# One pool of eight PSUM banks, scores in one block, and a gather product from split parts

## The reference

```python
x = _layernorm(x + attention(x, adj, adj, Wq, bq, Wk, bk, Wv, bv, Wo, bo))
# second layer, per head: h is x
Wh = jnp.einsum('bni,hoi->bhno', h, W) + bW[None, :, None, :]
e = jnp.einsum('bhno,hop->bhnp', Wh, attn)
scores = jnp.einsum('bhnp,bhmp->bhnm', e, Wh)
A_mat = jnp.tanh(jnp.where(adj[:, None, :, :], scores, 0.0))
hp = jax.nn.relu(jnp.einsum('bhnm,bhmo->bhno', A_mat, Wh))
cat = jnp.transpose(hp, (0, 2, 1, 3)).reshape(hp.shape[0], hp.shape[2], -1)
ha = cat @ A_w.T
hf = h @ fc_w.T
coeff = jax.nn.sigmoid(hf @ g1_w.T + ha @ g2_w.T + gbias)
x = _layernorm(x + hf * coeff + ha * (1.0 - coeff))
```

## Time and profile before

| | |
|---|---|
| median of 3 runs | 1156.95 us (1155.82 to 1157.34) |
| the profiled execution | 1157.57 us, of which the span is 1155.8 |
| granted TensorE clock, mean | 0.991 |
| TensorE busy | 1123.6 us (97%), 9756 matmul records |
| weight loads busy | 912.6 us (79%) |
| VectorE busy | 697.1 us (60%) |
| ScalarE busy | 511.6 us (44%) |
| GpSimd busy | 255.2 us (22%) |

### The profile page before, as it was taken

The page is one execution under the profiler, slowest core; times in us unless marked ns, Lnnn a source line. Parts: engine busy times, 40 slices in busy tenths (PEclk is TensorE's granted clock), DMA queues, the critical chain, the costliest instruction groups (busy, mean ns, idle before and its releaser), DMA issues.

```text
span 1155.8 us, 24597 instructions
## 1 busy us (share of the span) xinstructions
PE 1123.6 (97%) x9756; PEld 912.6 (79%) x9756; DVE 697.1 (60%) x1321; ACT 511.6 (44%) x908; POOL 255.2 (22%) x232
## 2 busy tenths in 40 slices
PE   6899999999999999999999999999999999999996
PEld 5778888787887878888787888878788787887774
DVE  6655665757556675665757566575765667566543
ACT  4444363534536253453625436353453625445241
POOL 1622131222212222131122213122221222211100
PEclk9999999999999999999999999999999999999998
DMA  7001000010000001000010100001000100100000
GB/s 248 16 7 41 19 22 20 18 40 18 25 29 24 19 18 40 18 20 19 18 40 18 40 18 20 19 18 40 18 21 24 33 19 18 40 19 3 1 19 18
DMA packets 26699, 32.58 MB, mean 28 GB/s; under 512 B 4400, under 2 KB 23344, under 8 KB 26288
## 3 DMA queue, kind: packets, MB, share of 16 engines
q1 hardware_dynamic: 26672, 32.19, 8.5%
HBM read 23.80 MB, written 8.39 MB: 28 GB/s over the span
## 4 chain that ended last, share of the span: by engine, by line
PE 94%; DVE 2%; POOL 2%; ACT 1%; issue 0%; DMA 0%; POOLq 0%; DVEq 0%; SPq 0%
PE bankB L344 20%; PE bankB L345 19%; PE bankB L346 19%; PE bankA L344 6%; PE bankB L550 5%; PE bankA L345 5%; PE bankA L346 5%; PE bankB L534 5%; PE bankA L448 3%; PE bankA L461 3%; PE bankA L475 2%; PE bankB L598 1%; PE bankA L501 1%; POOL aw_hi L1121 0%; DVE hf L1043 0%
## 5 line engine op out<-in xcount | busy, mean ns | idle before, releaser
L750 ACT ACTIVATE T<-bankB 128x512 f32<-128x512 f32 x128 | 76.5, 598 | 131.0 <-PE bankB L346 131.0
L777 ACT ACTIVATE cat_hi<-bankB 128x512 fp32r<-128x512 f32 x128 | 76.6, 598 | 129.3 <-PE bankB L346 129.3
L868 DVE SCALAR_TENSOR_TENSOR cat_lo<-bankB,cat_hi 128x512 fp32r<-128x512 f32 x128 | 86.4, 685 | 51.2 <-ACT cat_hi L777 50.2
L1148 POOL TENSOR_TENSOR probs<-probs,den 128x512 f32<-128x512 f32 x64 | 72.5, 1143 | 173.9 <-DVE den L957 173.9
L344 PE MATMUL bankB<-hT_lo,g_hi 128*128 128x512 f32 x256 | 108.3, 423 | 0.2 <-ACT res L796 0.2
L344 PE MATMUL bankB<-U_lo,wt_hi 128*128 128x512 f32 x256 | 101.4, 396 | 1.8 <-DVE U_lo L868 0.3
L345 PE MATMUL bankB<-hT_hi,g_lo 128*128 128x512 f32 x256 | 100.6, 393 | 0.0
L345 PE MATMUL bankB<-U_hi,wt_lo 128*128 128x512 f32 x256 | 100.1, 391 | 0.0
L346 PE MATMUL bankB<-U_hi,wt_hi 128*128 128x512 f32 x256 | 99.8, 390 | 0.0
L345 PE MATMUL bankB<-cat_hi,aw_lo 128*128 128x512 f32 x256 | 99.7, 390 | 0.0
L346 PE MATMUL bankB<-hT_hi,g_hi 128*128 128x512 f32 x256 | 99.7, 390 | 0.0
(11 more groups left out here) (143 smaller groups left out, 2640.3 us busy)
## 6 DMA issues: line engine op xcount, KB each, us to landing
y<-in_x SPq DMA_DIRECT2D x16, 512.0 KB, 3.5
out<-res SPq DMA_DIRECT2D x16, 512.0 KB, 3.0
x_raw<-in_xT SPq DMA_DIRECT2D x15, 512.0 KB, 3.3
W_nat<-in_Wn SPq DMA_DIRECT2D x1, 1028.0 KB, 6.4
attn_nat<-in_attn SPq DMA_DIRECT2D x1, 1024.0 KB, 8.7
adjS_u<-in_adjS SPq DMA_DIRECT2D x32, 32.0 KB, 2.8
raw_A<-in_AwT SPq DMA_DIRECT2D x1, 1024.0 KB, 8.5
x_second<-in_xT SPq DMA_DIRECT2D x1, 512.0 KB, 10.6
```

The lines of the kernel that those rows point to most:

```text
L750: take(act.activation(T[:, n % DC, n // DC, :], bank[:], ACT.Copy), "B", f"T{n}")
L777: act.activation(cat_hi[:, n, :], bank[:], ACT.Relu).then_inc(cat_hi_ready, 1)
L868: return dve.scalar_tensor_tensor(out=out, in0=bank, scalar=bias, in1=hi.bitcast(F32), op0=op, op1=ALU.subtract)
L1148: pool.tensor_tensor(view, view, den[:, j, :].unsqueeze(2).to_broadcast([P, NG, S]), ALU.mult) \
```

## The change

All eight banks are one pool, with lists of tiles and banks for each kind of turn (`FIRST`, `BODY`, `LAST`). The scores of a turn stand in one block after T0 (`scores`). The gather no longer multiplies f32 `Abuf` by f32 `h`: after the mask, ScalarE makes `A_hi` and VectorE `A_lo`; ScalarE makes `h_hi` and GpSimd `h_lo` at the end of the turn before; and `gathered_half` makes three fp32r matmuls of 256 columns for each one of before. All eight of its tiles come in a row after both `values` and the transposes, and attention stands behind them. `dense` now takes the low weights and the high weights with the high data for all terms first, and the products with the low data last; `then` is a wait in between. `h` is normalized in place of `y`, so the next load of `y` waits for hT and `h_lo`. The attention tiles of both column chunks share a bank. In the opening, three matmuls on zeros (`warm_up`) stand first, the scores come ahead of M1, two G products stand inside attention, ScalarE makes the late weights' high parts, and GpSimd's sum of x and bias follows the probabilities. In the last turn `h_fc` 1 stands ahead of the gather and `gate_h` ahead of the heads.

```diff
-BANKS = 4
+BANKS = 8
...
-SCORES_FROM = 1
-EXP_AFTER = (4, 5, 7)
+EXP_AFTER = (1, 3, 5, 7)
+LAST_IN_BANK = {False: ("probT1", "probT2", "probT3", "v1"), True: ("probT0", "probT1", "probT2", "probT3")}
+SPLIT_ORDER = ("G0", "G1", "G2", "G3", "G4", "G5", "G6", "W0", "W1", "W2", "W3", "G7", "FC")
...
+BODY = ("T0:4 score0:0 score1:1 score2:2 score3:3 T1:5 T2:6 T3:7 T4:4 T5:5 T6:6 T7:7 hf0:4 adj0:5 adj1:6 v0:0 v1:1 "
+        "probT0:2 probT1:3 probT2:0 probT3:1 U000:7 U001:4 U010:5 U011:6 U100:2 U101:3 U110:0 U111:1 attn0:7 attn1:4 "
+        "hf1:5 cat0:6 cat1:2 cat2:3 cat3:7 y0:0 y1:1 cat4:4 cat5:5 cat6:6 cat7:7 ha0:4 ha1:5 z0:6 z1:7 hT0:2 hT1:3 ")
+TURN = listed(BODY + "q0:0 q1:1 k0:2 k1:3 R0:6 R1:7")
+LAST_BUT_ONE = listed(BODY)
...
+        A_hi = at("A_hi", [P, NP, H2, S], F32R, r_cat + 16384)
+        A_lo = at("A_lo", [P, NP, H2, S], F32R, r_cat + 20480)
...
+            def dense(out, terms, first=True, last=True, then=None):
+
+
+                for n, (w, d, wsel, dsel) in enumerate(terms):
+                    pe.matmul(out, wsel(w[1]), dsel(d[0]), start=first and n == 0, stop=False)
+                    pe.matmul(out, wsel(w[0]), dsel(d[0]), start=False, stop=False)
+                if then is not None:
+                    then()
+                for n, (w, d, wsel, dsel) in enumerate(terms):
+                    ins = pe.matmul(out, wsel(w[0]), dsel(d[1]), start=False, stop=last and n == len(terms) - 1)
                 return ins
...
+            def warm_up():
+
+                pe.wait_ge(zeros_ready, 1)
+                for n in range(3):
+                    pe.matmul(BANK[BANKS - 1][:], hf[:, 0, 0:P], hf[:, 0, :], start=True, stop=True)
...
+            def scores(g):
+                for n in ("q0", "q1", "k0", "k1"):
+                    await_taken(pe, "A", n, g)
+                for two in (0, 2):
+                    for j in range(two, two + 2):
                         claim(pe, "A", f"score{j}", g)
-                for b in graphs:
-                    for c in range(DC):
-                        for j in banks:
-                            rows = slice(HD * j, HD * j + HD)
-                            ins = pe.matmul(bank_of("A", f"score{j}")[c * S:c * S + S, b * S:b * S + S],
-                                            qT[rows, c, b * S:b * S + S], kT[rows, c, b * S:b * S + S],
-                                            start=True, stop=True)
-                            if b == NG - 1 and c == DC - 1:
-                                filled(ins, "A", f"score{j}")
+                    for b in range(NG):
+                        for c in range(DC):
+                            for j in range(two, two + 2):
+                                rows = slice(HD * j, HD * j + HD)
+                                ins = pe.matmul(bank_of("A", f"score{j}", g)[c * S:c * S + S, b * S:b * S + S],
+                                                qT[rows, c, b * S:b * S + S], kT[rows, c, b * S:b * S + S],
+                                                start=True, stop=True)
+                                if b == NG - 1 and c == DC - 1:
+                                    filled(ins, "A", f"score{j}", g)
...
+            def gathered_half(g, q2):
 
                 pe.wait_ge(A_ready, g * 2 + (q2 + 1))
+                pe.wait_ge(h_lo_ready, g + 1)
                 for c in range(DC):
                     for b in range(2):
                         claim(pe, "B", f"U{q2}{c}{b}", g)
                     carried(pe)
                     for q in range(2):
+                        p = 2 * q2 + q
+                        for n, (hs, As) in enumerate(((h_lo, A_hi), (h_hi, A_lo), (h_hi, A_hi))):
+                            for b in range(2):
+                                rows = slice(b * S, b * S + S)
+                                bank = bank_of("B", f"U{q2}{c}{b}", g)[:].rearrange("p (h q n) -> p h q n", h=H2, q=2)
+                                ins = pe.matmul(bank[:, :, q, :], hs[rows, p, c * P:c * P + P], As[rows, p, :, :],
+                                                start=n == 0, stop=n == 2)
+                                if q == 1 and n == 2:
+                                    filled(ins, "B", f"U{q2}{c}{b}", g)
...
             def heads_out(g, ns):
                 if 0 in ns:
-                    for q2, c, b in U_TILES[-BANKS:]:
-                        await_taken(pe, "B", f"U{q2}{c}{b}", g)
+                    pe.wait_ge(U_hi_ready, (g + 1) * len(U_TILES))
                 for n in ns:
                     bank = claim(pe, "B", f"cat{n}", g)
                     filled(dense(bank[:], [
                         (Wt, (U_hi, U_lo), lambda t, k=k: t[:, k, n * P:n * P + P], lambda t, k=k: t[:, k, n // DC, :])
-                        for k in range(DC)]), "B", f"cat{n}")
+                        for k in range(DC)], then=lambda: await_taken(pe, "B", "U111", g)), "B", f"cat{n}", g)
...
             def turn(A, B, more):
                 if B is None:
+                    warm_up()
                     queries(0)
                     keys(0)
-                    M1_products(range(2))
-                    for two in (0, 2):
-                        scores(0, range(two, two + 2), range(NG))
+                    scores(0)
+                    M1_products(range(H2 * DC))
                     values(0, 0)
-                    M1_products(range(2, H2 * DC))
                     probs_T(0, range(2))
                     G_products(range(4))
                     probs_T(0, range(2, JB))
                     values(0, 1)
                     G_products(range(4, 5))
-                    attention(0)
+                    attention(0, range(1))
+                    G_products(range(5, 7))
+                    attention(0, range(1, DC))
                     W_transposed()
                     project(0)
-                    G_products(range(5, H2 * DC))
+                    G_products(range(7, H2 * DC))
                     queries(1)
                     gate_weights()
                     h_T(0)
...
                 for n in range(KC):
                     T_tile(B, n)
+                    if A is not None and n == 0:
+                        scores(A)
                     if A is None and n == 1:
                         res_T(B - 1)
-                    if A is not None and 0 <= n - SCORES_FROM < 4:
-                        two, part = (n - SCORES_FROM) // 2 * 2, (n - SCORES_FROM) % 2 * (NG // 2)
-                        scores(A, range(two, two + 2), range(part, part + NG // 2))
                 h_fc(B, 0)
                 adj_scores(B)
-                gathered(B, 0)
-                if A is not None:
-                    values(A, 0)
-                gathered(B, 1)
-                if A is not None:
-                    probs_T(A, range(JB))
-                    values(A, 1)
+                if A is None:
+                    h_fc(B, 1)
+                    gathered(B)
+                    gate_h(B)
+                    heads_out(B, range(KC))
+                    h_a(B)
+                    gate_a(B)
+                    res_T(B)
+                    return
+                values(A, 0)
+                values(A, 1)
+                probs_T(A, range(JB))
+                gathered(B)
+                attention(A, range(DC))
                 h_fc(B, 1)
-                if A is not None:
-                    attention(A)
                 heads_out(B, range(KC // 2))
-                if A is not None:
-                    project(A)
+                project(A)
                 heads_out(B, range(KC // 2, KC))
                 h_a(B)
                 gate_h(B)
-                if A is not None:
-                    h_T(A)
+                h_T(A)
                 gate_a(B)
                 if more:
                     queries(A + 1)
                     keys(A + 1)
-                if more or A is None:
                     res_T(B)
 
...
             def adj_tanh(g):
                 for q2 in range(2):
+                    part = slice(2 * q2, 2 * q2 + 2)
                     bank = await_tile(act, "B", f"adj{q2}", g)
-                    ins = act.activation(Abuf[:, 2 * q2:2 * q2 + 2, :, :],
-                                         bank[:].rearrange("p (q h n) -> p q h n", q=2, h=H2), ACT.Tanh)
-                    take(ins, "B", f"adj{q2}")
-
-            def U_high(g, q2):
-                if q2 == 0 and later(g):
+                    ins = act.activation(Abuf[:, part, :, :], bank[:].rearrange("p (q h n) -> p q h n", q=2, h=H2),
+                                         ACT.Tanh)
+                    take(ins, "B", f"adj{q2}", g)
+                    act.wait_ge(A_masked, g * 2 + (q2 + 1))
+                    act.activation(A_hi[:, part, :, :], Abuf[:, part, :, :], ACT.Copy).then_inc(A_hi_ready, 1)
+
+            def h_high(g):
+                act.wait_ge(h_ready, g * NP + NP)
+                act.activation(h_hi[:], y[:], ACT.Copy).then_inc(h_hi_ready, 1)
...
                     early()
```

(72 more changed lines are left out.)

381 lines of the change are left out of this document (195 added, 186 removed).

## The result

The changed kernel takes **1115.24 us** (median of four runs, 1113.58 to 1116.31) against 1156.86 us of the kernel before beside it (1155.82 to 1157.34): a ratio of 0.964, 95% interval 0.9623 to 0.9657. The prediction said 1118.0, between 1106 and 1142. The profiled execution has a span of 1113.1 us, 42.7 less than before.

A forecast was written before the change was run, and what follows sets the result against it. TensorE, with 94% of the chain, was taken as the bound. 15 turns at 2.07 us (31) plus opening 6.5, `Abuf` wait 0.8 and last turn 0.8 sum to 39.1 us less: 1118 us, range 1106 to 1142.

The forecast's parts named there:

- Scores: In each turn, 64 score matmuls in one block instead of four pieces: gain 1.07 us a turn, between 0.9 and 1.2.
- Gather: In each turn, split products of 64-row halves run in pairs, 0.12 us a step: gain 0.9 us a turn.
- in series: In the gather, split products of the two halves don't overlap: 46 us more, 1164 us; chance 0.10.
- partly: In the gather, the halves overlap only partly, 0.18 us a pair: 1141 us; chance 0.06.
- Order of the middle: Between adjacency and heads, less switching of matmul kind: gain 0.1 us a turn, between 0.2 and a loss of 0.1.
- The cover: In each turn, values and transposes hide the A copies; U copies come 1.1 and 0.3 us ahead of need.
- the copies become the bound: In each turn, U copies 1.3 us later make the heads product wait 1 us: 1133 us; chance 0.10.
- lost cover: In each turn, without values and transposes before the gather, TensorE would wait 3.5 us for the A halves.
- The opening: Before the first T tile, net gain 6.5 us, with 3 and 10 as the ends.
- Step (2): In the opening, attention's 2.51 us stall mostly goes: banks no longer shared, two G products put into it.
- Step (3): In the opening, given back: later values and attention, some 4 us of TensorE idle, up to 2 us at lower clock.
- The last turn: From gather to the end, hf1 and gate's h part fill waits, haT split loses cover: net gain 0.8 us.

The follow-up runs named there:

- This order: Changed kernel with the whole gather ahead of values and transposes: 1204.43 us; with other banks for values and transposes, 1160.78 us.
- the kernel with the gap filled: Changed kernel with matmuls on zeros (56 small, then three of 512 columns) between keys and scores in the opening, where TensorE waited 4.4 us: 1122.28 us.

## Why the prediction was right

**The bound and the steady turn: right, 0.4 us a turn too small.** Forecast 66.6 us, measured 66.26.
- Scores: forecast 1.07, measured 1.19 in place, and 1.21 when only this part is undone. The size was missed a little: the single block takes 1.95 in the loop, while the row it was sized from (2.05, in the opening) holds its own edge.
- Gather: the step of a pair is 0.12 as taken from the earlier trace rows, and the halves do run side by side. 24 pairs and their edges take 3.07, forecast 2.98: the first step and the last are 0.22, not 0.12. The rivals "in series" (1164) and "partly" (1141) are out, as the pairs show. The weight loads overlap too, two of 0.19 us every 0.12 us. The Trainium skill, TensorE: Matmul & The Clock Gate, LDWEIGHTS, says that rows don't shorten a load; the trace agrees (0.19 us with 64 rows, 0.188 with 128), and here it costs nothing.
- Order of the middle: forecast 0.1, measured 0.4. 0.17 of it is the values in one row, as read from the earlier trace rows. The other 0.23 is attention, 1.64 before and 1.41 after from its start to the next product. I had counted no gain there and no run isolates it, so its cause stays open.

**The cover: right in kind.** The margins of the U copies are 0.9 and 0.4 us, forecast 1.1 and 0.3, and the rival "the copies become the bound" (1133) didn't come. The sentence on lost cover was wrong in size: I wrote that TensorE would wait the whole 3.5 us for A, and it waits 1.57, since the first half's products fill the time of the second half's copies. But losing the cover costs 3.0 us a turn in all, because PT is then late as well (0.98), and 0.4 stay unexplained. This order does end slower than the kernel before, but only half of its loss is the wait that I named.

**The opening: right in most parts, 1.7 us too large.** GpSimd's split no longer holds the norm, attention doesn't stall (it is in two parts without a bracket), and the low stretch at 56 is gone. Step (2) gave the shared banks as the reason of the 2.51 us in attention, and no row shows that. The bracket says "issue", and a packet of 16 KB of instructions was in at 37.43, 1.5 us before TensorE went on at 38.90; in turn 1 of the changed kernel the packet is in at 60.93 and TensorE goes on at 62.28. So it was probably a wait for instructions, which no run tested. Not counted was the low stretch 0.4 us behind it, which had cost the transposes of W 1.6 us. Step (3) failed in size. It named the 4 us of idle time and "up to 2 us" for the lower level, yet the first T tile was put at 56.1; it came at 57.9, and the low stretch alone cost 1 us in the scores and 2 in M1. Not seen at all was the wait for instructions in turn 1 (1.14 us): with it the first full turn saves 1.8 us (69.5 to 67.7), where 2.07 and 0.8 for `Abuf` were forecast.

**The last turn: forecast 0.8, measured 1.8.** From its adjacency product to its last transposes it takes 39.9 us instead of 41.1 (1.2), and the T tiles go on 0.5 us sooner after the previous group's last transposes.

**The sum.** 0.4 us a turn too little, 1.7 too much in the opening, 1.0 too little at the end: 1118 forecast, 1115.2 measured. The span came out 3.6 us below its forecast (1113.1 for 1116.7) and the median 2.8, since it lies 2.1 above the span and not 1.2. The misses in opposite directions hid each other in part, which is luck.

## What to carry to other kernels

Where TensorE is the bound, count its changes of kind (here 0.40 us for each block of small matmuls put between dense ones) and put small matmuls in one block; and put the work that needs no fresh copy between a product and the product that needs its copies, for the same instructions in another order were 45 us slower. An engine's queue holds more than the wait that the profile names: moving one late load gave no gain clear of the noise, until the next instruction in the same queue that waited for a load was moved as well (5 us together). Before reading a gap as a wait for data, check whether it stays at the same instruction when code ahead of it is added or removed.

## What the runs showed of the hardware that I had not expected

- Matmuls on different halves of the rows overlap even when the program doesn't put them side by side: 48 records in 3.07 us in either order.
- Matmuls of 32 rows and 64 columns cost 0.015 us a record in the scores (128 in 1.95 us), where neighbours alternate between two sets of 32 rows, two banks and two halves of the output's partitions. They cost 0.058 when all have the same rows, the same bank and the same output (the 103 records of the filling before the clock fell, in 6.0 us). Which of these makes the difference was not tried.
- The granted clock fell to 0.50 at 18.7 us in the kernel with the gap filled, while TensorE was never without a matmul, in a row of small ones.
- TensorE waits 1.0 to 1.8 us for its own instructions where 256 of them are used up within 2 us, in turn 1. In the loop that follows it does so on the first pass at most (0.3 to 0.8 us), and not in turns 3 to 14.
